# Layer 0 of a two-layer convolution kernel: strip normalised in halves, input loaded ahead of the pair's wait, real frequencies as sums and differences

## The reference, cut to what matters

```python
def _L0_conv_ref(x, ...):                       # x is already group-normalised
    hidden = einsum('bchw,oc->bohw', x, w_hidden) + b_hidden      # 64 -> 384
    hidden = depthwise_conv_3x3(hidden, w_dw) + b_dw
    q, k, v = jnp.split(hidden, 3, axis=1)                        # 128 channels each
    q_fft = jnp.fft.rfft2(_to_patches(q))                         # patches of 8 x 8
    k_fft = jnp.fft.rfft2(_to_patches(k))
    out = _from_patches(jnp.fft.irfft2(q_fft * k_fft, s=(8, 8)))
    out = (out - mean_c) / sqrt(var_c + 1e-05) * ln_w + ln_b      # over channels
    return einsum('bchw,oc->bohw', v * out, w_proj) + b_proj
x = x + _L0_conv_ref(_gn(x), ...)
x = x + _L1_conv_ref(_gn(x), ...)               # involution, softplus, 3x3 conv, softplus
```

## Time and profile before

| what | value |
|---|---|
| median of 3 runs | 10036.34 us (10029.1 to 10041.79) |
| the profiled execution | 10034.93 us, span 10033.1 us |
| mean granted clock of TensorE | 0.988 |
| TensorE busy | 9128.4 us (91%) |
| ScalarE, VectorE, GpSimd busy | 6973.9, 6036.7, 4896.1 us |
| DMA traffic | 718.26 MB, mean 72 GB/s |

### The profile page before, as it was taken

One profiled execution on the slowest core, in us unless ns is written; L12 is line 12 of the kernel. 1 busy time (PEld: TensorE's weight loads), 2 busy tenths in 40 slices (PEclk: granted clock), 3 DMA queues, 4 the chain that ended last, 5 costly groups with the idle time before them and its releaser, 6 DMA issues. The chain is left out here.

```text
span 10033.1 us, 169594 instructions
## 1 busy us (share of the span) xinstructions
PE 9128.4 (91%) x58854; PEld 5045.6 (50%) x58854; DVE 6036.7 (60%) x7784; ACT 6973.9 (70%) x9573; POOL 4896.1 (49%) x2751
## 2 busy tenths in 40 slices
PE   1999999999999999999999999999868888888888
PEld 0666666666666666666665555555322222222222
DVE  4555555555555555555555454544558888888887
ACT  1777777777777777777776767767217777777777
POOL 1334433343344344433433333333118888888888
PEclk9999999999999999999999999999989999999999
DMA  6122222222222222222212111111764444444444
GB/s 129 47 60 55 48 57 56 56 50 55 60 55 47 59 56 55 50 55 60 55 39 48 39 48 39 47 40 39 162 157 105 104 104 104 104 104 104 104 104 102
DMA packets 619184, 718.26 MB, mean 72 GB/s; under 512 B 44324, under 2 KB 578138, under 8 KB 595142
## 3 DMA queue, kind: packets, MB, share of 16 engines
q1 hardware_dynamic: 618950, 714.70, 30.2%
HBM read 549.65 MB, written 164.89 MB: 71 GB/s over the span
## 5 line engine op out<-in xcount | busy, mean ns | idle before, releaser
L550 PE MATMUL banks<-w_hi,hi_lo 128*128 128x256 f16 x18432 | 2380.6, 275 | 132.5 <-issue 80.9
L550 PEld LDWEIGHTS banks<-w_hi,hi_lo 128*128 128x128 f16 x18432 | 1795.2, 99 | 556.4 <-issue 209.9
L508 POOL TENSOR_TENSOR u_im<-q_im,k_swap 128x512 f32<-128x512 f32 x512 | 706.4, 1380 | 2136.2 <-ACT q_im L706 2082.8
L1292 POOL TENSOR_TENSOR part_sum<-part_sum,prod 128x1024 f32<-128x1024 f32 x660 | 1559.8, 2363 | 261.7 <-DVE prod L1570 218.8
L1327 PE MATMUL banks<-z,conv_w 128*128 128x512 f32 x3140 | 1523.4, 614 | 0.0
L688 ACT ACTIVATE qk<-banks,inv_wscale 128x512 f32<-128x512 f32 x1024 | 689.9, 687 | 1040.8 <-PE banks L550 1028.4
L818 DVE TENSOR_TENSOR u<-q_re,banks 128x512 f32<-128x512 f32 x512 | 351.0, 686 | 1717.1 <-ACT q_re L712 1341.5
L511 POOL TENSOR_TENSOR u<-u,u_im 128x512 f32<-128x512 f32 x512 | 649.7, 1269 | 1338.8 <-DVE u L818 1338.8
L567 PE MATMUL banks<-hi_lo,w_hi 128*128 128x512 f16 x4608 | 1085.7, 381 | 13.9 <-DVE tmp L887 13.9
L550 PE MATMUL banks<-w_lo_pair,hi_pair 128*128 128x256 f16 x6144 | 1012.0, 274 | 0.0
L498 POOL TENSOR_TENSOR hl_all<-xn,hi_all 64x1280 f16<-64x1280 f32 x258 | 793.2, 3074 | 241.2 <-ACT hi_all L681 219.2
(11 more groups left out here) (210 smaller groups left out, 16400.3 us busy)
## 6 DMA issues: line engine op xcount, KB each, us to landing
xr<-in_x_dram SPq DMA_DIRECT2D x258, 640.0 KB, 9.1
xb<-y_scratch SPq DMA_DIRECT2D x268, 320.0 KB, 4.8
xa<-y_scratch SPq DMA_DIRECT2D x270, 256.0 KB, 5.3
x_res<-in_x_dram SPq DMA_DIRECT2D x258, 256.0 KB, 4.2
out_dram<-res SPq DMA_DIRECT2D x258, 256.0 KB, 5.1
y_scratch<-ys SPq DMA_DIRECT2D x256, 256.0 KB, 4.1
yc<-y_scratch SPq DMA_DIRECT2D x256, 256.0 KB, 6.0
xs<-in_x_dram SPq DMA_DIRECT2D x92, 512.0 KB, 7.1
```

Of the source, the lines that this page charges most:

```text
L508: nc.gpsimd.tensor_tensor(u_im[:], q_im[:], k_swap[:], ALU.mult).then_inc(u_made, 1)
L550: r = pe.matmul(out, px, w, start=n == 0, stop=n == 13)
L1292: nc.gpsimd.tensor_tensor(part_sum[:], prod[0][:] if n == 0 else part_sum[:], prod[n + 1][:], ALU.add)\
```

## The change

1. `q_split` and its two copies go: the setup makes other matrices, so that the frequencies which are real by themselves need no treatment of their own. Their forward rows become half the sum and half the difference of the two old rows (`sums`, `differences`), `idft` gets matching rows (`own_sign`, `idft_other`), and `imag_sign` is 1 there. The setup gains four short loads, one clear on GpSimd and twelve short VectorE operations.
2. `normed` is cut into two halves of 128 columns. The first half of a strip is made one group earlier (group 3 of the strip before, ahead of that group's `v_copy`), the second where the whole was. `xn_made` now counts halves. The first half waits for `low_made` in place of `stacks_ready`.
3. SyncE asks for a strip of `x` one strip further ahead, in front of the wait for the pair.
4. `averages` is eight matmuls of 32 output partitions and one column each in place of one.
5. `run` gives the last iteration a loop of its own, with `last` set, since there is no further strip to load and normalise.

```diff
@@ setup, SyncE
+                    sp.wait_ge(v_cleared, 1)
+                    for part in range(2):
+                        for half in range(2):
+                            lo, src = C * part + 32 * half, C * (1 - part) + 2 * half
+                            sp.dma_start(idft_other[lo:lo + 2], A["idft"][src:src + 2]).then_inc(transforms_loaded, 16)
-                sp.wait_ge(transforms_loaded, 16 * 24)
+                sp.wait_ge(transforms_loaded, 16 * 28)
@@ setup, GpSimd
-                    last = nc.gpsimd.memset(t[:, KQ:KV], 0.0)
+                    nc.gpsimd.memset(t[:, KQ:KV], 0.0)
+                last = nc.gpsimd.memset(idft_other[:], 0.0)
@@ setup, VectorE
+                v.wait_ge(transforms_loaded, 16 * 28)
+                then(v.memset(own_sign[:], 1.0))
+                for half in range(2):
+                    then(v.memset(own_sign[C + 32 * half:C + 32 * half + 2], -1.0))
+                    for part in range(2):
+                        lo = C * part + 32 * half
+                        then(v.memset(imag_sign[lo:lo + 2], 1.0))
+                then(v.scalar_tensor_tensor(idft[:], idft[:], own_sign[:, 0:1], idft_other[:], ALU.mult, ALU.add))
+                then(v.tensor_tensor(sums[:], dft[:, 0, 0:2], dft[:, 1, 0:2], ALU.add))
+                then(v.tensor_tensor(differences[:], dft[:, 0, 0:2], dft[:, 1, 0:2], ALU.subtract))
+                then(v.tensor_scalar(dft[:, 0, 0:2], sums[:], 0.5, None, ALU.mult))
+                then(v.tensor_scalar(dft[:, 1, 0:2], differences[:], 0.5, None, ALU.mult))
@@ run
-                with eng.Fori(start, NB) as i:
-                    body(i, False, False, None)
+                with eng.Fori(start, NB - 1) as i:
+                    body(i, False, False, None, False)
+                with eng.Fori(NB - 1, NB) as i:
+                    body(i, False, False, None, True)
@@ layer 0, SyncE
                     for b in range(2):
+                        if not (last and b == 1):
+                            of, halves_before = i * 2 * R + (b + 2) * R, i * 4 + 2 * b + 2
+                            if not first:
+                                of, halves_before = sp.snap(of), sp.snap(halves_before)
+                            sp.wait_ge(xn_made, halves_before)
+                            load(of, b)
                         if not (first and b == 0):
-                            sp.wait_ge(xn_made, normed_before)
-                            load(of, 1 - b)
...
                             sp.wait_ge(pair_ready, pairs_before)
                             load_res(of_res, 1 - b)
                             store(to, 1 - b)
@@ layer 0, TensorE
-                    pe.matmul(b_v[:, 0:2], pair_avg[:], tmp[:, 0:2, :].rearrange("p a i -> p (a i)"), start=True, stop=True)\
-                        .then_inc(gn_answered, 1)
+                    for q in range(4):
+                        for a in range(2):
+                            made = pe.matmul(b_v[32 * q:32 * q + 32, a:a + 1], pair_avg[:, 32 * q:32 * q + 32], tmp[:, a, :],
+                                             start=True, stop=True)
+                    made.then_inc(gn_answered, 1)
...
-                                pe.wait_ge(q_split, i * 8 + k)
+                                pe.wait_ge(q_copied, i * 8 + k)
@@ layer 0, ScalarE
-                def normed(s, b):
-                    act.wait_ge(x_loaded[b], (s - b) * 16 + 32)
-                    act.wait_ge(par_ready, s + 1)
-                    if not isinstance(s, int) or s >= 1:
-                        act.wait_ge(stacks_ready, s + 0)
-                        act.wait_ge(hi_made, s + 0)
-                    act.activation(xn[:, :, 0:SL], xr[b][:].rearrange("p s w -> p w s"), ACT.Identity, bias=par[b][:, 1:2],
-                                   scale=par[b][:, 0:1]).then_inc(xn_made, 1)
+                def normed(s, b, half):
+                    if half == 0:
+                        act.wait_ge(x_loaded[b], (s - b) * 16 + 32)
+                        act.wait_ge(par_ready, s + 1)
+                        if not isinstance(s, int) or s >= 1:
+                            act.wait_ge(low_made, s * 2)
+                            act.wait_ge(hi_made, s + 0)
+                    cols = slice(W // 2 * half, W // 2 * half + W // 2)
+                    act.activation(xn[:, cols, 0:SL], xr[b][:, :, cols].rearrange("p s w -> p w s"), ACT.Identity,
+                                   bias=par[b][:, 1:2], scale=par[b][:, 0:1]).then_inc(xn_made, 1)
...
-                    act.wait_ge(q_copied, i * 8 + k)
-                    act.copy(by_block(q_re[C:C + 2, :]), b_q[C:C + 2])
-                    act.copy(by_block(q_re[C + 32:C + 34, :]), b_q[C + 32:C + 34]).then_inc(q_split, 1)
...
+                        if k % 4 == 3 and not (last and k == 7):
+                            normed(i * 2 + (k // 4 + 2), k // 4, 0)
                         if k % 4 == 0:
-                            normed(i * 2 + (k // 4 + 1), (k // 4 + 1) % 2)
+                            normed(i * 2 + (k // 4 + 1), (k // 4 + 1) % 2, 1)
@@ layer 0, VectorE
-                    v.wait_ge(xn_made, s + 1)
+                    v.wait_ge(xn_made, s * 2 + 2)
...
-                    v.wait_ge(q_split, i * 8 + k)
+                    v.wait_ge(q_copied, i * 8 + k)
```

More of the change, by code:

```diff
@@ L79, in build_program @@
         imag_sign = sb("imag_sign", [P, 2])
+        own_sign = sb("own_sign", [P, 1])
         mean_w = sb("mean_w", [P, P])
@@ L105, in build_program @@
             wmax = tsb("wmax", [P, 4])
+            idft_other = tsb("idft_other", [P, P])
+            sums = tsb("sums", [P, 2])
+            differences = tsb("differences", [P, 2])
             loaded = ph.enter_context(nc.semaphore("weights_loaded"))
@@ L366, in build_program @@
             q_copied = tsem("q_copied")
-            q_split = tsem("q_split")
             q_im_ready = tsem("q_im_ready")
@@ L411, in run @@
             def run(eng, body, tail=None):
-                body(0, True, NI > 1, None)
+                body(0, True, NI > 1, None, False)
                 start = 1
@@ L415, in run @@
                     with eng.Fori(start, n * IT - 2) as i:
-                        body(i, False, True, None)
+                        body(i, False, True, None, False)
                     with eng.Fori(n * IT - 2, n * IT - 1) as i:
-                        body(i, False, n < NI - 1, n)
+                        body(i, False, n < NI - 1, n, False)
                     start = n * IT - 1
-                with eng.Fori(start, NB) as i:
-                    body(i, False, False, None)
+                with eng.Fori(start, NB - 1) as i:
+                    body(i, False, False, None, False)
+                with eng.Fori(NB - 1, NB) as i:
+                    body(i, False, False, None, True)
                 if tail:
@@ L445, in load_stats, with body @@
                                      A["x"][:, bass.ds(row + R * h, R), :]).then_inc(xs_loaded, 16)
-                def body(i, first, stats, image):
+                def body(i, first, stats, image, last):
                     if stats:
@@ L456, in body @@
                     for b in range(2):
+                        if not (last and b == 1):
[4 more added lines that the diff above has]
+                            load(of, b)
                         if not (first and b == 0):
-                            to, of, of_res = i * 2 * R + b * R, i * 2 * R + (b + 1) * R, i * 2 * R + (b + 1) * R + 1
-                            normed_before, pairs_before = i * 2 + b, i * 4 + 2 * b
+                            to, of_res, pairs_before = i * 2 * R + b * R, i * 2 * R + (b + 1) * R + 1, i * 4 + 2 * b
                             if not first:
-                                to, of, of_res = sp.snap(to), sp.snap(of), sp.snap(of_res)
-                                normed_before, pairs_before = sp.snap(normed_before), sp.snap(pairs_before)
-                            sp.wait_ge(xn_made, normed_before)
-                            load(of, 1 - b)
+                                to, of_res, pairs_before = sp.snap(to), sp.snap(of_res), sp.snap(pairs_before)
                             sp.wait_ge(pair_ready, pairs_before)
@@ L635, in body @@
                                 pe.wait_ge(qk_copied, i * 16 + (2 * k - 1 + t // 2))
-                            last = conv(b, b_qk[t // 2][:, KQ * (t % 2):KQ * (t % 2) + KQ], 4 * cg + t)
+                            made = conv(b, b_qk[t // 2][:, KQ * (t % 2):KQ * (t % 2) + KQ], 4 * cg + t)
                             if t % 2:
-                                last.then_inc(qk_conv, 1)
+                                made.then_inc(qk_conv, 1)
                             if t == 1 and k % 2 == 0 and not (first and k < 4):
@@ L762, in _ @@
                 act.wait_ge(buffers_zeroed, 1)
-                normed(0, 0)
+                normed(0, 0, 0)
+                normed(0, 0, 1)
                 high_parts(0)
+                normed(1, 1, 0)
```

## The result

The kernel after takes 9717.14 us (median of 4, 9711.99 to 9722.63) against 10036.5: a ratio of 0.9682, interval 0.9666 to 0.9699. The forecast of 9755 us had the direction, and in layer 0 the waits that would go and the loop that would no longer fetch its instructions. Its terms were too small: the time lies 38 us under the forecast and 21 us under the lower end of its range, 9738.

The account below looks back on a forecast made before the run. TensorE was taken to set layer 0's time. From the profiled 10034.9 us, -112.0 - 102.6 - 68.1 - 3 + 4.3 gave 9753.5, and 1.4 more for the median 9755 us; its own range 9738 to 9780, 8 in 10 9738 to 9866.

Parts of the forecast that it names:

- What bounds layer 0: Layer 0: TensorE sets the time, busy 102.58 of 105.21 us an iteration; every other engine has slack.
- The place in the code, -112: Last loop of layer 0: moved to touch 7 instruction blocks, not 8, it stops fetching; 16 jumps x 7.0 us, -112.0.
- The shift: All four loop starts: what the launch puts ahead of the program may shift them alike, by about -15 to +55 instructions.
- The two waits, -102.6 and -68.1: TensorE's once-per-strip waits in layer 0: `sq` (groups 1, 5) goes, -102.6 us; `u` (groups 3, 7) goes but for 5.7, -68.1.
- Halves and early loads, 0: Loads ahead of the pair: requests leave at the same moments, one strip further ahead, so data is there; price 0.
- The remark on what the old order would do: Group 3's first half `xn`: with the request at the pair, data lands near 4063.9 and is found barely or not.
- Image changes, -3: End of each image: VectorE reaches its place for `tmp` about 1.1 us sooner, 3 images, -3 us.
- Setup, +4.3: Before layer 0: four row loads 2.0 us and twelve short operations 2.3 us, +4.3 us, bounds 0 and 7.
- rival 1: Last loop still fetches: 15 jumps x 7.0 us, +105, giving 9860 us; chance 0.12.
- (2): A stall replaces one removed, the VectorE chain being tight: the `u` wait stays, 9823 us, partly 9790; chance 0.13.
- (4): Clock: TensorE without idle time is granted less than 1.00; at 0.99 +65 us, 9820; chance 0.02.
- The slower rival (3): All four loops need a block too many and fetch: 55 jumps x 7.0 = 385 us, 10140 us; chance 0.03.

Follow-up runs that it names:

- 2: Kernel before with only the averages as eight small matmuls: 9919.18 us, ratio 0.9887.
- 3: Kernel after with the averages as one matmul again: 9824.87 us, ratio 0.9793.
- 7: Kernel after with 75 more instructions (waits already met) on TensorE ahead of its first loop: 10070.1 us, ratio 1.0029.
- 4: Kernel after with the strip normalised in one piece and the old order of loads, copies still out: 9716.37 us, ratio 0.9683.
- 5: Kernel after with the two `q_split` copies and old matrices back, halves and early loads kept: 9801.04 us, ratio 0.9765.
- 6: Kernel after with the old order of loads (strip s+1 asked for ahead of the pair's wait), halves kept: 9945.68 us, ratio 0.9912.
- 9: Kernel after with halves and the old order of loads, but `xs` asked for behind `xr`: 9719.4 us, ratio 0.9684.
- 1: Kernel before run once more with no edit: 10033.6 us.

## Why the prediction was right or wrong, point by point

- **What bounds layer 0.** Right. TensorE is now busy 102.29 us of 102.29, at a granted clock of 1.00.
- **The place in the code, -112.** Right as a mechanism, and shown both ways (2, 3) and by making it worse (7). The term was too small: it was taken from one iteration of 112.17 us, and the mean over the last loop is 112.62. The starts in the kernel after are 85, 80, 75, 70, four more than I counted. So the first lies just outside the 15 to 81 that the trace had shown to be free, and it was free all the same. The shift that I said the trace allows, -15 to +55, was also wrong at its upper end: beyond +17 the fourth loop, at 238, would have touched 7 blocks and been free too. The rule by which every loop would have paid (the Trainium skill, "Runtime: NRT & Kernel Launch", "Instruction fetch mechanics": only two blocks are held) does not hold for this engine here: the kernel after jumps back 55 times and moves 62 instruction packets in all. The 128 KiB in blocks of 16 KiB that the same section of the Trainium skill gives this engine, eight blocks, agree with 7 free and 8 not. q8 fell to 62 packets, not to near 80, since a jump fetched nine.
- **The two waits, -102.6 and -68.1.** Right in which edit removes which (4, 5): the copies take both, a half would take `sq` alone. (0.8 x 127 is 101.6; the 102.6 of the sum is the 103.4 less the tail's 0.8.) The size is the step that failed: the sum priced a wait by the idle time that the profile gives it. But a matmul's modelled end overlaps the next one. Without a wait the variance starts 0.21 us after the last convolution matmul has started, whose own length is 0.27 (4053.98 and 4054.19 above); with the wait it was 1.07 (4086.59 to 4087.66). For the inverse it was 1.60 from the start of the transform to its own (4064.77 to 4066.37) and is 1.01 without the wait (4045.97 to 4046.98 in after). The lines of before that the rows lack:

```profile
4086.59 0.27 PE L550 MATMUL banks<-w_lo_one,hi_ind 128*128 128x256 f16 x1
...
4064.77 1.09 PE L606 MATMUL banks<-qk,dft 64*32 64x512 f32 x16
```

So the wait of 0.80 cost 0.86, that of 0.52 some 0.58 (half of the 1.15 in experiment 5), and the iteration got 2.90 us shorter, not 2.67: 15 us over the layer.

- **Halves and early loads, 0.** Right: 4 is as fast as after. The remark on what the old order would do was wrong in size: it added 9.4 us to the end of the pair's statistics, "barely or not", and the expectation of 6 made up to 28 us of it. It is 229. From the end of the statistics to `xn` it is 13.8 us without `xs` and 18.0 with it, since SyncE first issues `x_res`, the store and, in most iterations, `xs` (6, 9). A half takes 2.86 us, not 2.65, which cost nothing.
- **Image changes, -3.** -7: TensorE's wait for `tmp` fell by 1.3 us each (13.9 to 10.1 in all), and the other waits of these iterations with it. The eight averages cost nothing visible behind it, as said: with one matmul (experiment 3) the three take 5.9, 5.9 and 7.2.
- **Setup, +4.3.** +3.2 between these two profiles. The first convolution matmul starts at 214.0 to 215.5 us in the three profiles of the old kernel and at 216.4 to 217.9 in five with the new setup (after, 3, 4, 6, 9).
- **The sum and its range.** Of the 323 us between the two profiles the forecast had 281: 15 from the price of waits, 7 from the jump, 4 from the image changes, 1 from the setup, and 13 between two profiles in stages whose code is the same; about 1 is left over. The 13 lie in code that the change doesn't touch, and even without them the time would be some 9730, under the range. The spread of whole executions of after is 10.7 us. The lower end stood 17 us under the forecast, though the jump rested on one row, a low one, and the two waits on the idle column alone. That is what the range should have held.
- **Rivals.** The last loop doesn't fetch (rival 1), no stall took the place of one removed (2), the clock is 1.00 with no idle time (4). The slower rival (3) exists: experiment 7 comes near it, with 41 jumps that pay instead of 55.

## What to carry to other kernels

Compare the same loop body at its several places in the program: equal work and a longer iteration with waits of "issue" and instruction packets is a matter of code address, and a few added or removed instructions decide over more than a percent. Price a wait by start-to-start distances with and without it, not by the idle column, and take the mean over all its occurrences. When an operation is moved earlier, look for what stands in the DMA queue ahead of its input, not only for when its input is requested.

## What the runs showed of the hardware

- A TensorE loop of 1,656 instructions ran without fetching from every start tried between 15 and 130 (modulo 256) and fetched at every jump from those tried between 150 and 242 (150, 155, 160, 238, 242): nine packets of 16.4 KB and 6.8 to 9.0 us on average, most of it idle, the rest matmuls at the lower clock. Why the cost differs with the place (one wait of 5.4 to 7.0 us in the first three loops of 7, two of 1.7 to 3.4 in before, 1 and 3) is open; in both forms the granted clock of the iteration fell to 0.97 or 0.98.
- At a start of 145 the loop fetched once, at its second jump, and then stayed. That wasn't followed up.
- `xn` by halves costs 2 x 2.86 = 5.72 us against 5.30 whole, 0.4 us more for the pair.
